# An AdaLN, attention and mixture-of-experts block on one core: bias products on 64 rows of the array, and the attention tile's matrix work ordered by the shape of the array tiles

## The reference, cut to what matters

```python
c = x @ cond_w[cat] + cond_b[cat]                 # 16 categories, one per sequence
q, k, v = lora_linear(c) ...                      # 16 heads of 16
attn = softmax(q k^T / 4 + slope * (kpos - qpos)) @ v
x2 = x + c + rezero * lora_linear(attn)
z = lora_out(x2; A[lang], B[lang]) + lang_embed[lang]   # rank 16, 4 languages
ys = geglu(z @ Ws1 + bs1) @ Ws2 + bs2             # shared feed-forward
w = softmax over the top 2 of ((z @ Wr + br) / 1.5)     # 12 experts
yr = sum over chosen e of w[e] * (geglu(z @ We1[e] + be1[e]) @ We2[e] + be2[e])
out = x2 + ys + yr
```

## Time and profile before

| | |
|---|---|
| runs, median (lowest to highest) | 955.81 us (953.32 to 957.62) |
| profiled execution | 958.14 us |
| its span | 956.2 us |
| mean granted clock of TensorE | 0.978 |
| chain of work that ended last | PE 93%, DVE 3%, all else 4% of the span |
| busy: PE, DVE, POOL, ACT | 920.3, 516.2, 402.4, 295.6 us |

### The profile page before, as it was taken

The page is one execution under the profiler, slowest core; times in us unless marked ns, Lnnn a source line. Parts: engine busy times, 40 slices in busy tenths (PEclk is TensorE's granted clock), DMA queues, the critical chain, the costliest instruction groups (busy, mean ns, idle before and its releaser), DMA issues.

```text
span 956.2 us, 28042 instructions
## 1 busy us (share of the span) xinstructions
PE 920.3 (96%) x9693; PEld 698.1 (73%) x9694; DVE 516.2 (54%) x1154; ACT 295.6 (31%) x783; POOL 402.4 (42%) x511
## 2 busy tenths in 40 slices
PE   7889999999999999899999899999999999999995
PEld 6667777777777777656666677777777777777774
DVE  2575555555555566556775245555454555545452
ACT  0333333333333333243232223232332323233230
POOL 2133333333333332100000366666666666666652
PEclk8999999999999999889999799999999999999998
DMA  8434445545454432015742122222222222222221
GB/s 269 114 98 151 151 151 151 151 151 151 151 151 151 151 86 79 1 51 176 220 171 63 68 30 35 31 30 34 28 35 28 34 30 31 33 28 35 28 32 23
DMA packets 49005, 85.60 MB, mean 90 GB/s; under 512 B 7267, under 2 KB 27555, under 8 KB 48835
## 3 DMA queue, kind: packets, MB, share of 16 engines
q1 hardware_dynamic: 33634, 68.76, 23.1%
q0 software_dynamic: 13888, 15.13, 11.9%
q10 hardware_dynamic: 1440, 1.16, 0.5%
HBM read 68.48 MB, written 16.55 MB: 89 GB/s over the span
## 4 chain that ended last, share of the span: by engine, by line
PE 93%; DVE 3%; ACT 1%; issue 1%; DMA 1%; ACTq 1%; DVEq 0%; POOL 0%
PE ps L1380 21%; PE ps L1368 15%; PE ps L1106 7%; PE ps L1284 6%; PE ps L1273 4%; PE ps L1363 4%; PE ps L1201 4%; PE ps L1159 4%; PE ps L1117 4%; PE ps L1085 3%; PE ps L1147 3%; PE ps L1175 3%; PE ps L1205 2%; PE ps L1187 2%; PE ps L1352 2%; PE ps L1139 2%
## 5 line engine op out<-in xcount | busy, mean ns | idle before, releaser
L1380 PE MATMUL ps<-arena,stage 128*128 x900 | 208.5, 382 | 0.0
L1380 PEld LDWEIGHTS ps<-arena,stage 128*128 128x128 f32 x900 | 166.7, 192 | 20.0
L470 POOL DMA_INDIRECT out_dram<-stage,to_row x75 | 120.6, 1608 | 129.0 <-DVE stage L1015 126.1
L1368 PE MATMUL ps<-token_rows,token_rows_T 64*128 64x128 f32 x1800 | 163.6, 301 | 0.0
L627 ACT ACTIVATE stage<-ps 128x384 f32<-128x384 f32 x150 | 65.5, 488 | 281.9 <-PE ps L1368 281.9
L1368 PEld LDWEIGHTS ps<-token_rows,token_rows_T 64*128 64x128 f32 x1800 | 119.9, 189 | 15.2
L995 DVE COPY token_rows<-ps 128x128 f32<-128x128 f32 x75 | 21.9, 291 | 169.3 <-PE ps L1353 169.3
L462 POOL DMA_INDIRECT token_rows<-gated_rows,from_row x75 | 75.0, 1000 | 87.6 <-DVE to_row L907 64.9
L386 POOL TENSOR_TENSOR arena<-arena 128x256 f32<-128x256 f32 x32 | 23.2, 726 | 195.9 <-DVE arena L749 195.9
L1106 PE MATMUL ps<-arena 128*128 128x128 f32 x512 | 75.8, 292 | 5.4 <-ACT arena L523 5.4
L1000 DVE TENSOR_TENSOR stage<-ps,stage 128x384 f32<-128x384 f32 x150 | 75.9, 548 | 2.3 <-ACT stage L627 2.3
(11 more groups left out here) (169 smaller groups left out, 1437.2 us busy)
## 6 DMA issues: line engine op xcount, KB each, us to landing
stage<-in_we_dram SPq DMA_DIRECT2D x36, 512.0 KB, 4.5
arena<-in_cond_w_dram SPq DMA_DIRECT2D x64, 256.0 KB, 2.8
arena<-in_we_dram SPq DMA_DIRECT2D x12, 768.0 KB, 4.3
arena<-in_x_both_dram SPq DMA_DIRECT2D x32, 256.0 KB, 2.6
arena<-in_L_cond_bias_dram SPq DMA_DIRECT2D x64, 64.0 KB, 2.7
out_dram<-arena SPq DMA_DIRECT2D x32, 128.0 KB, 1.7
be_bc<-in_be_rows_dram SPq DMA_DIRECT2D x13, 192.0 KB, 2.7
gated_rows<-token_rows POOLq DMA_DIRECT2D x2, 1152.0 KB, 10.1
```

The costliest lines, as they stand in the source:

```text
L470: pool.indirect_dma_start(out_rows, bass.IndirectOffsetOnAxis(to_row[:, t:t + 1], 0), y_sb[t % YR], None, compute_op=ALU.add).then_inc(d_a ...
L1368: last = mm(ps[:, 2 * g + hf, at], w1x[s % 2][64 * g:64 * g + 64, j * CW + hf * P:j * CW + (hf + 1) * P], s_rowT[s % 2][64 * g:64 * g + 64 ...
L1380: last = mm(ps[:, 4 + s % 2, 0:D], actT_sb[s % 2][:, hf, j * P:(j + 1) * P], arena[:, ds(e * E2 + (NJ * hf + j) * D, D)], start=(hf == 0 a ...
```

## The change

Three things change. (1) The language rows are kept in two versions, one with the 32-row groups of the first half set to zero and one with those of the second, so a bias product takes 64 rows of `w1b` instead of 32; the unwanted 32 rows meet zeros. The number of products stays; in the routed stage VectorE makes two masked copies where it made one. (2) The score's position products are done per 64 columns, in the shape of the products that follow. (3) The attention tile's steps are put in another order: `project` is split into k, q and v; v goes directly before `attend`, `condition` and the second merge directly behind it; `low_rank` and `row_transpose` run two tiles late instead of one, in PSUM bank 6, which they now share with the merges, so `low_rank` waits for the merge's copy. VectorE, ScalarE and GpSimd follow that order.

```diff
-        langB = sb("lang_rows", [P, B], bf16)
+        langB = sb("lang_rows", [P, 2, B], bf16)
...
             def tile_steps(i, odd, last=False):
...
                 keep(i - 1, not odd)
+                if not (isinstance(i, int) and i < 2):
+                    keep_low(i - 2)
...
# DVE, tile_steps
-                    v_spread(i + 1, not odd)
-                if not first:
+                if not isinstance(i, int) or i > 1:
+                    t_mask(i - 2)
+                if not isinstance(i, int) or i > 0:
                     x2_add(i - 1, not odd)
                 pT_copy(i)
-                if not first:
-                    t_mask(i - 1)
+                if one_more:
+                    v_spread(i + 1, not odd)
+                if not isinstance(i, int) or i > 1:
+                    logit_sum(i - 2)
                 normalize(i)
...
             def rowT_copy(t, s):
                 dve.wait_ge(rowT_ps, t + 1)
                 V.tensor_copy(s_rowT[s % 2], ps[:, 7, 0:P])
-                V.tensor_copy(s_langT[s % 2], ps[:, 7, P:2 * P]).then_inc(rowT_sb, 1)
+                for hf in range(2):
+                    last = V.tensor_scalar(s_langT[s % 2][hf], ps[:, 7, P:2 * P], col["half"][:, hf:hf + 1], None, ALU.mult)
+                last.then_inc(rowT_sb, 1)
...
+            def project_k(i):
+                pe.wait_ge(cT_sb, i + 1)
+                if not isinstance(i, int) or i > 0:
+                    pe.wait_ge(v_sb, i)
+                transposed(1, 4, 0).then_inc(k_ps, 1)
+
+            def project_q(i):
+                transposed(0, 5, D).then_inc(q_ps, 1)
+
+            def project_v(i):
+                pe.wait_ge(k_sb, i + 1)
...
-                for g in range(4):
-                    mm(ps[:, g, 0:256], ali[32 * g:32 * g + 2, 0:P], ali[32 * g:32 * g + 2, P:P + 256], start=True,
-                       stop=False)
+                for b in range(2):
+                    for g in range(4):
+                        mm(ps[b * S:(b + 1) * S, g, 0:256], ali[32 * g:32 * g + 2, b * S:(b + 1) * S],
+                           ali[32 * g:32 * g + 2, P:P + 256], start=True, stop=False)
...
-            def low_rank(i):
+            def low_rank(i, merges):
                 pe.wait_ge(x2T_sb, i + 1)
+                pe.wait_ge(merge_sb, merges)
+                if not isinstance(i, int) or i > 0:
+                    pe.wait_ge(tT_sb, i)
...
# PE, tile_steps
                 if merge_a:
-                    merge(*merge_a)
+                    merge(*merge_a, rows=i - 2 if late else None)
                 if one_more:
-                    project(i + 1)
-                if not first:
+                    project_k(i + 1)
+                    project_q(i + 1)
+                if late:
+                    low_rank(i - 2, merged)
+                if not isinstance(i, int) or i > 0:
                     output(i - 1)
                 prob_transpose(i)
-                if not first:
+                if late:
+                    row_transpose(i - 2)
+                if not isinstance(i, int) or i > 0:
                     x2_transpose(i - 1, not odd)
-                if merge_b:
-                    merge(*merge_b)
-                if not first:
-                    low_rank(i - 1)
+                if one_more:
+                    project_v(i + 1)
                 attend(i, odd)
-                if not first:
-                    row_transpose(i - 1)
                 if two_more:
                     condition(i + 2, odd)
+                if merge_b:
+                    merge(*merge_b, rows=i - 1 if late else None)
...
# hidden
-                           w1b[32 * r:32 * r + 32, unit * P:(unit + 1) * P],
-                           sh_lang[32 * r:32 * r + 32, half, :].unsqueeze(2).to_broadcast([32, U // S, S]),
+                           w1b[64 * g:64 * g + 64, unit * P:(unit + 1) * P],
+                           sh_lang[64 * g:64 * g + 64, half, hf, :].unsqueeze(2).to_broadcast([64, U // S, S]),
...
# first_layer
-                    for r in range(4):
-                        mm(ps[:, r, at], w1bx[s % 2].bitcast(bf16)[32 * r:32 * r + 32, at],
-                           s_langT[s % 2][32 * r:32 * r + 32, :], start=True, stop=False)
+                    for hf in range(2):
+                        for g in range(2):
+                            mm(ps[:, 2 * g + hf, at], w1bx[s % 2].bitcast(bf16)[64 * g:64 * g + 64, at],
+                               s_langT[s % 2][hf][64 * g:64 * g + 64, :], start=True, stop=False)
```

More of the change, by code:

```diff
@@ L193, in adaln_attn_moe @@
         s_wide = [cut(2 * P) for _ in range(2)]
-        s_langT = [cut(P // 2).bitcast(bf16) for _ in range(2)]
+        s_langT = [[cut(P // 2).bitcast(bf16) for _ in range(2)] for _ in range(2)]
         cut = Cut(ltT)
@@ L446, in _ @@
             keep(NT - 1, True)
+            for i in range(NT - 2, NT):
+                keep_low(i)
             pool.wait_ge(kept_t, NT)
@@ L587, in unit_copy @@
                 copy(sh_x[:, half, :], ltT[:, ds(u * U, U)])
-                copy(sh_lang[:, half, :], langB[:, ds(u * (U // S), U // S)]).then_inc(shx_ok, 1)
+                copy(sh_lang[:, half, :, :], langB[:, :, ds(u * (U // S), U // S)]).then_inc(shx_ok, 1)
             def shared_gelu(u):
@@ L788, in logit_sum, with tile_steps @@
                                 lrow.rearrange("p l n -> p n l"), AX.X, ALU.add).then_inc(lg_sb, 1)
-            def tile_steps(i, odd, first=False):
+            def tile_steps(i, odd):
                 one_more, two_more = not isinstance(i, int) or i + 1 < NT, not isinstance(i, int) or i + 2 < NT
@@ L813, in _ @@
             c_add(1, True)
-            tile_steps(0, False, first=True)
+            tile_steps(0, False)
             router_consts()
@@ L1093, in c_transpose, with transposed @@
                 last.then_inc(cT_ps, 1)
-            def project(i, first=False):
+            def transposed(w, bank, at):
+                for m in range(KC):
+                    for k in range(KC):
+                        last = mm(ps[:, bank, at + m * P:at + (m + 1) * P], wm[w][:, k, m * P:(m + 1) * P], cT[:, k, :],
+                                  start=(k == 0), stop=(k == KC - 1))
+                return last
+            def project_k(i):
                 pe.wait_ge(cT_sb, i + 1)
-                if first:
-                    pe.wait_ge(s_mrgc, 1)
                 if not isinstance(i, int) or i > 0:
-                    pe.wait_ge(k_sb, i)
                     pe.wait_ge(v_sb, i)
-                def transposed(w, bank, at):
-                    for m in range(KC):
-                        for k in range(KC):
-                            last = mm(ps[:, bank, at + m * P:at + (m + 1) * P], wm[w][:, k, m * P:(m + 1) * P], cT[:, k, :],
-                                      start=(k == 0), stop=(k == KC - 1))
-                    return last
-                transposed(1, 4, 0)
-                if first:
-                    pe.wait_ge(s_mrgc, 2)
+                transposed(1, 4, 0).then_inc(k_ps, 1)
[3 more added lines that the diff above has]
+                pe.wait_ge(k_sb, i + 1)
                 wv = [wm[2][:, k, :].rearrange("p (h two d) -> p two h d", two=2, d=HD) for k in range(KC)]
@@ L1119, in project @@
                                 start=(k == 0), stop=(k == KC - 1))
-                last.then_inc(kv_ps, 1)
-                if first:
-                    pe.wait_ge(s_mrgc, 3)
-                transposed(0, 5, D).then_inc(q_ps, 1)
+                last.then_inc(v_ps, 1)
             def score(i):
@@ L1192, in row_transpose, with merge @@
                 pe.wait_ge(t_sb, i + 1)
-                tr(ps[:, 7, 0:P], trow.rearrange("p d l r -> p (d l r)"), ident).then_inc(tT_ps, 1)
-            def merge(n, j, arrived):
+                tr(ps[:, 6, 0:P], trow.rearrange("p d l r -> p (d l r)"), ident).then_inc(tT_ps, 1)
+            def merge(n, j, arrived, rows):
                 pe.wait_ge(d_stage[j], arrived)
+                if rows is not None:
+                    pe.wait_ge(tT_sb, rows)
                 if not isinstance(n, int) or n > 0:
@@ L1207, in merge, with tile_steps @@
                 last.then_inc(merge_ps, 1)
-            def tile_steps(i, odd, first=False, merge_a=None, merge_b=None):
+            def tile_steps(i, odd, merged, merge_a=None, merge_b=None):
                 one_more, two_more = not isinstance(i, int) or i + 1 < NT, not isinstance(i, int) or i + 2 < NT
+                late = not isinstance(i, int) or i > 1
                 score(i)
@@ L1241, in _ @@
             c_transpose(0)
-            project(0, first=True)
+            pe.wait_ge(s_mrgc, 1)
+            project_k(0)
+            pe.wait_ge(s_mrgc, 3)
+            project_q(0)
+            project_v(0)
             condition(1, True)
```

59 lines of the change are left out of this document (33 added, 26 removed).

## The result

The changed kernel takes **885.94 us** (884.88 to 889.81, four runs) beside 956.71 us (953.32 to 957.98) of the kernel before on the same chip: 0.927 times, with a 95% interval of 0.924 to 0.931. The prediction was 884.7. The profiled execution took 885.9, its span is 884.0.

The account below looks back on a forecast made before the run. The prediction took TensorE's own sequence to bound the kernel. Its terms, 39.4 + 14.4 + 17.3 = 71.1 us, took the median from 955.8 to about 884.7 us; forecast 875 to 893, range with rival 1 868 to 898.

Parts of the forecast that it names:

- routed stage: 75 routed tiles: bias on 64 rows makes a group 0.60 us and saves 0.53 a tile, 39.4 us in all.
- shared stage: Hidden products of a unit take 2.29 us instead of 3.40; 13 of 16 units counted, 14.4 us.
- attention stage: Fewer changes of shape per tile after reordering, less a new wait in the loop's odd tiles: 17.3 us gained.
- tiles 27 to 30: Last attention tiles: fewer changes of shape and no `x2T` wait, 9.15 us each, 5.2 gained in all.
- Price of a change of shape: On TensorE: 0.11 us until the array is empty plus up to 0.10 for an uncovered f32 load, 0.155 on average.
- Rival 3: The 0.11 goes with change of type, not shape, or bf16 on 64 rows keeps its own shape: 951 us; chance 0.05.
- VectorE's second copy: Routed tile: a second masked copy costs 0.28 us, hidden in 1.07 of slack, leaving 0.79.
- eleven pairs: Attention loop: 2.2 us saved per pair of tiles less the new wait, net 0.34 a pair, 3.8 for eleven.
- wait behind the merge: Loop's odd tile: low-rank waits for ACT's merge copy behind POOL's cut, 1.76 us idle plus 0.10 load, 1.86.
- Rival 4: Slower: the clock falls in the attention loop behind the new wait; twelve falls give 966 us; chance 0.03.
- Rival 1: Bias pairs on 64 rows stream no faster than f32: 12.4 us less gained, 897 us; chance 0.12.
- Rival 2: The loop's wait for the merge's copy isn't there: 11 x 1.86 us more gained, 864 us; chance 0.10.

Follow-up runs that it names:

- the part alone: Each part run separately: routed bias 919.65 us and shared bias 939.46 us in the kernel before; attention stage, kernel after with both biases on 32 rows, 938.32 us.
- experiment 5: Kernel after with the routed bias back on 32 rows, one masked copy, all twelve bias products of a tile ahead of the f32 ones: 876.37 us.
- experiment 9: Kernel after with the score's position products as before, four of 128 columns instead of eight of 64: 889.33 us.
- experiment 1: Kernel before with only the routed stage's bias products on 64 rows, and VectorE's second masked copy: 919.65 us.
- experiment 2: Kernel before with only the shared stage's bias products on 64 rows: 939.46 us.
- experiment 3: Kernel after with both bias products back on 32 rows, so the attention stage's part alone: 938.32 us.
- experiment 4: Kernel after with ScalarE's copy of an odd tile's first merge waiting for the second of POOL's four counted cut steps, not the fourth: 870.95 us.
- experiment 8: Kernel after with four more masked copies on VectorE in each routed tile, into spare memory: 919.29 us.
- Experiment 6: Kernel after with all twelve routed bias products of a tile, on 64 rows, ahead of the 24 f32 ones: 879.60 us.

## Why the prediction was right, point by point

| term | predicted | changed kernel's trace | the part alone, its own stage in its trace | the part alone, whole time |
|---|---|---|---|---|
| routed stage | 39.4 | 38.3 | 38.2 | 37.8 |
| shared stage | 14.4 | 15.2 | 15.7 | 18.0 |
| attention stage | 17.3 | 17.1, and 1.6 at the start | 15.9 | 19.1 |
| sum | 71.1 | 72.2 of span | 69.8 | 74.9 |

The trace's terms are differences between the two traces at the same place: the first `hidden`, 406.7 and 388.0; the first routed transposes, 532.7 and 498.8; the end.

- **That the number was met within 1.2 us is in part luck.** The 1.6 of the start and the 2 to 3 of the clock, both below, are in the measured gain and not in the prediction. Without them the three terms gave some 3 us less than predicted: the routed group's size and tiles 27 to 30 fell short, the loop gave more.
- **What bounds the kernel**: TensorE's own sequence did, and what was taken from it in the routed stage no other engine took back. Exceptions after the change are the odd tile of the loop, which POOL's cut sets, and the score of tiles 27 to 30, which waits for VectorE.
- **Price of a change of shape**, 0.155 on average: experiment 5 gives 0.16 for those of the routed tile, experiment 9 0.13 a tile for the one of the position products. For the other changes in the attention tile it was not measured one by one; what the trace of the kernel before shows of the parts of the price stands behind this list. In the routed group the reasoning was right and the size a little off: a group takes 0.61, not 0.60, so 4.90 and not 4.87. That is 2.2 us of the term; the part alone gave 1.6 less than predicted, 37.8 for 39.4. Rival 3 is out by experiments 1 and 2.
- **VectorE's second copy** lay in its slack, as said. It cost 0.33 and not 0.28, and 0.6 of slack is left where the prediction had 0.79.
- **Shared stage**: the unit came out at 2.28 for 2.29. From the first sorting product on (L1304 before, L1332 after), the 13 units gave 14.3 in the part alone (106.5 to 92.2 us), as predicted (14.4), but 12.8 in the changed kernel. Ahead of it, where the prediction counted nothing because of VectorE's chain, there were 1.5 alone and 2.4 in the changed kernel, in part perhaps the clock's. What is missing behind it lies at the stage's end: VectorE's last add of a result (L942) started 3.3 us after the one before it, where these adds are else 1.7 apart and where it was 1.7 before. In the experiments it is 1.8 to 3.2, and 2.0 in the kernel of experiment 9, which is the changed one at this place, so the edit alone doesn't set it. What releases it the profile doesn't show, and it stays open.
- **Attention stage**: tiles 1 and 2 gave 2.5 (2.4 predicted), the first pair 2.5 (2.7), eleven pairs 4.5 (3.8), the stage's end 3.3 (3.2). The wait behind the merge was 1.43 with its load, not 1.86: from L1113 to L1203 it is 3.32 in the odd tile (201.75 to 205.07) and 1.89 in the even one. POOL's cut starts 0.60 after the score and not 0.86, since from the even tile's last merge products to the next score it takes 0.81 (198.05 to 198.86) where another step followed them after 0.57. It goes with the turn of the loop, which lies there: 0.17 of it is idle time that the profile puts down to issue, and from an odd tile's merge to the even tile's score it is 0.58. That moved 0.24 from the odd into the even tile, and the pair nearly stayed: 23.9 for 23.94 (24.28 less 0.34). Of the stage's end, 3.3, about 1.2 is there because the clock stayed up: with a fall of 3.4 us, in experiment 3, it gave 2.2.
- **The step that failed**: tiles 27 to 30, 9.15 predicted and 9.32 measured, 4.3 us gained for 5.2. The working took `low_rank`, attention and the row transpose from between one score and the next and did not ask what is late next. It is VectorE's `onorm`, which the score waits for; condition alone doesn't cover it. This is 0.5 of the 0.9 that are missing. Of the rest 0.3 was never there to gain: tile 30 took 10.15 before and not 10.45, which the prediction took for all four.
- **The start**, 1.6: tile 1's first f32 score product began at 36.3 before and 34.7 after, and in the kernels of the experiments anywhere from 33.3 to 36.1. In experiment 1, whose attention stage is that of the kernel before, it was 34.4. So it is luck and not the change's.
- **The clock**: the prediction kept both falls. After there was one, 17 us less at the lower level. By experiment 2, where 10.2 us less of it gave 3.8, and by experiment 3's 1.2 at the attention stage's end, I estimate 2 to 3 us of the 70.8. The run with the mean clock 0.977, like the kernel before's 0.978, took 889.81; the three at 0.986 to 0.988 took 885.6 on average. Rival 4 rested on the fall of the kernel before at 399.0, to 0.50, which stood 0.2 us ahead of the end of a wait of 1.77 us. It did not come: no fall from 22.6 to 500.5, and none in the loop behind the new wait in any of the six traces that have it. But what stood against it was weak: the wait of tile 3, behind which the clock stayed at 1.00 in the kernel before, had a fall behind it in experiment 1.

**The parts of the price, in the trace of the kernel before.** Where the shape stays and the type changes, on the whole array, nothing is lost: the eight L1284 products from 474.68 to 476.19 and the bf16 product behind them (476.41) start 0.215 to 0.217 apart. The f32 load behind a bf16 product is hidden there: the LDWEIGHTS of L1284 starts at 428.98, with the bf16 L1308 (428.97) and 0.16 ahead of its own product (429.14). Where the shape changes, the load starts no earlier than its product (706.64), 0.17 behind the first bias product. Timeline of PEld:

```profile
706.47 0.10 PEld L1363 LDWEIGHTS ps<-token_rows,token_rows_T 32*128 32x128 bf16 x4 [0.33 <-issue]
706.64 0.52 PEld L1368 LDWEIGHTS ps<-token_rows,token_rows_T 64*128 64x128 f32 x8
```

Of the 0.17 the bias products' own 0.057 leaves the 0.11; that the array becomes empty in it is the prediction's reading, and no run shows more than the gap. For the uncovered f32 load the longest and the median product are 0.102 us apart on 128 columns, 0.051 on 64 and 0.025 on 32 (ns, shortest/median/longest):

```profile
L1117 PE MATMUL ps<-arena x272: 272/273/324, 101.6 to 296.7; 128*64 128x128 f32 x136
L1205 PE MATMUL ps<-stage,ba x384: 272/273/298, 106.7 to 289.8; 128*32 128x128 f32 x192
```

The f32 loads themselves take 0.19, 0.14 and 0.11 us on 128, 64 and 32 columns (L1368, L1117, L1205), the bf16 loads of the bias 0.09 (L1363). So the 0.05 and 0.02 that the prediction took for f32 are there; the 0.02 for bf16 is not: of the bias products none is longer than the others before (L1363, 224 to 226 ns), and after the first pair is by 0.01 (L1392, 226 for 216).

Rival 1 is out by the routed tile (5.04 was its bound). Rival 2 was wrong as a forecast, since the wait was there, but three quarters of what it priced could be had: 15.0 of 20.5 us, experiment 4.

## What to carry to other kernels

Look at which shape of the array each group of products takes, and count the changes: here one costs 0.11 us until the next group starts and up to 0.10 for a weight load that nothing hides. Products of the same shape belong together; here it mattered less whether small products run side by side (0.02 us a tile) than how often the shape goes there and back (0.63 a tile). Where a step is moved behind a wait, follow the wait to the operation that really frees the buffer: a copy waited for a whole chain of five operations here of which it needed three, and one number gave 15 us. And a moved step leaves a gap: ask which wait it covered.

## What the runs showed of the hardware that was not expected

- Besides the first and the last part of the program, the lower clock came at the same two places in nearly all kernels, the end of the attention stage (not in the changed kernel and experiment 8) and the start of the routed stage, but for 3.4 us (at the first in experiment 3) to 17 us (there in experiment 1). A difference of 7.7 us (0.8%) between two runs of one kernel went with the mean clock. The same wait of 2.3 us in tile 3 had no fall behind it in the kernel before and one of 3.4 us in experiment 1.
- Behind bf16 products on 64 rows the first f32 pair took 0.053 longer than the next ones, against 0.102 behind bf16 products on 32 rows, as if half of the f32 load were hidden: its LDWEIGHTS starts 0.05 ahead of its product there (719.88, L1397), and together with it before (706.64, L1368). Experiment 6 took two of the three away, and the tile fell by 0.106, twice 0.053.
- Eight position products of 2 rows and 64 columns took 0.11 to the score, four of 128 columns 0.22 (360.66 to 360.77 in the changed kernel, 362.80 to 363.02 in experiment 9): twice as many instructions in half the time, once their shape is that of what follows.
- A masked copy out of PSUM costs VectorE 0.26 in a row of its kind (starts of L1010 in the changed kernel, 702.83 and 703.09), a plain one 0.20 or 0.21 (L1008 to L1010 there, 702.62 to 702.83; L996 to L1000 before).
